# Attention written out without registers, and the routing of twelve of sixteen token blocks laid between its maximum chunks

## What is computed

```python
mod = (silu(c) @ wmod)                      # sa, ca, ga, sb, cb, gb, one row of 256 per batch
ga, gb = sign * max(|.|, 0.25)
h = layernorm(x) * (1 + ca) + sa
q, k, v = einsum(h, W_qkv)                  # 16 heads of 16
attn = softmax(causal(q @ k.T) / 4)
x = x + ga * ((attn @ v) @ W_o)
h = layernorm(x) * (1 + cb) + sb
probs = sigmoid(h @ router_w.T)             # 8 experts, widths 4 x 256 and 4 x 512
topw, sel = top_k(probs, 2)                 # weights divided by their sum + 1e-20
y = sum over the 2 experts of topw * (square(relu(h @ w1_e)) @ w2_e)
out = x + gb * y
```

## Time and profile before

| | us |
|---|---|
| median of three runs (lowest, highest) | 3000.57 (2999.84, 3001.91) |
| the profiled execution, its own time | 2998.05 |
| the span of the profiled execution, first to last instruction | 2996.4 |
| attention, first maximum chunk to last context | 245 to 2038 |
| routing stage | 2040 to 2445 |
| busy share of the span: PE, DVE, ACT, POOL | 87%, 75%, 57%, 21% |

### The profile page before, as it was taken

The page is one execution under the profiler, slowest core; times in us unless marked ns, Lnnn a source line. Parts: engine busy times, 40 slices in busy tenths (PEclk is TensorE's granted clock), DMA queues, the critical chain, the costliest instruction groups (busy, mean ns, idle before and its releaser), DMA issues. The chain is left out here.

```text
span 2996.4 us, 63588 instructions
## 1 busy us (share of the span) xinstructions
PE 2607.4 (87%) x16384; PEld 1391.3 (46%) x16384; DVE 2235.7 (75%) x5319; ACT 1718.0 (57%) x3557; POOL 643.7 (21%) x595
## 2 busy tenths in 40 slices
PE   6876999999999999999999999984566559999990
PEld 5761233333333333333333333323555559999990
DVE  6988988889788878887888988803666657777762
ACT  3650377767677667766776767782121227777770
POOL 2224111111100000000000000001454525565563
PEclk8995799999999999999999999996666669999995
DMA  4876535544530220220121120004444425555547
GB/s 152 284 274 184 186 138 175 183 153 161 184 121 29 70 70 10 72 70 28 51 69 37 41 69 13 9 15 154 146 159 141 148 79 81 89 95 90 88 76 239
DMA packets 229815, 332.44 MB, mean 111 GB/s; under 512 B 27472, under 2 KB 170064, under 8 KB 229456
## 3 DMA queue, kind: packets, MB, share of 16 engines
q1 hardware_dynamic: 165184, 200.83, 21.7%
q0 software_dynamic: 47376, 110.68, 14.2%
q10 hardware_dynamic: 16896, 16.78, 1.7%
HBM read 140.23 MB, written 187.20 MB: 109 GB/s over the span
## 5 line engine op out<-in xcount | busy, mean ns | idle before, releaser
L734 ACT ACTIVATE probs<-ps 128x512 f32<-128x512 f32 (+3 forms) x2560 | 1173.9, 540 | 612.4 <-PE ps L828 367.7
L763 DVE TENSOR_REDUCE early<-ps 128x1 f32<-128x512 f32 x1536 | 1005.0, 686 | 130.7 <-PE ps L806 111.2
L806 PE MATMUL ps<-ks,qs 96*128 96x512 bf16 (+3 forms) x2560 | 887.9, 364 | 58.1 <-POOL ks L697 30.6
L824 PE MATMUL ps<-qs,ks 99*128 99x512 bf16 (+3 forms) x2560 | 831.5, 351 | 30.6 <-ACT probs L734 19.1
L841 PE MATMUL ps<-probs,vs 128*32 128x512 f32 (+3 forms) x5120 | 601.2, 542 | 0.0
L806 PEld LDWEIGHTS ps<-ks,qs 96*128 96x128 bf16 x2560 | 248.0, 98 | 641.3 <-DVE early L763 227.3
L759 DVE CUSTOM_DVE_ANT_0 junk<-ps,causal 128x128 bf16<-128x128 f32 (+3 forms) x1024 | 487.6, 484 | 77.8 <-PE ps L806 66.2
L824 PEld LDWEIGHTS ps<-qs,ks 99*128 99x128 bf16 x2560 | 247.0, 98 | 329.2 <-ACT probs L734 196.0
L1413 POOL DMA_INDIRECT acc<-y,to x156 | 252.8, 1620 | 113.2 <-ACT y L1468 67.2
L1029 POOL MEMSET w_raw<- 128x2048 f32 x1 | 1.8, 1809 | 1177.7 <-POOLq L618 1177.7
L828 PE MATMUL ps<-ident_b,causal_b 128*128 128x128 bf16 x1024 | 215.3, 221 | 0.0
(11 more groups left out here) (177 smaller groups left out, 3232.9 us busy)
## 6 DMA issues: line engine op xcount, KB each, us to landing
rows_out<-empty POOLq DMA_DIRECT2D x129, 544.0 KB, 3.4
xg<-rows_out SPq DMA_DIRECT2D x39, 544.0 KB, 3.7
v_ones<-vt SPq DMA_DIRECT2D x16, 1024.0 KB, 6.1
vs<-v_ones SPq DMA_DIRECT2D x16, 1024.0 KB, 6.3
contexts<-ctx_out SPq DMA_DIRECT2D x64, 256.0 KB
q_parts<-parts SPq DMA_DIRECT2D x32, 384.0 KB, 3.8
k_parts<-parts SPq DMA_DIRECT2D x32, 384.0 KB, 4.4
qs<-q_parts SPq DMA_DIRECT2D x64, 192.0 KB, 3.1
```

The source lines that it names most:

```text
L734: nc.scalar.activation(probs[u % PB][:, h, q0:TB], bank(n % SB)[:, q0:TB], ACT.Exp, scale=SCALE).then_inc(exp_done[p], 1)
L763: nc.vector.tensor_reduce(early[:, h, t, k0 // CW:k0 // CW + 1], tile, AX.X, ALU.max).then_inc(max_done[p], 1)
L806: mm = nc.tensor.matmul(bank(4 + c % MS * (CW // 512), CW // 512)[:, m0:m0 + n], qs[p][0:STACK, h, t * P:(t + 1) * P], ks[p][0:STACK, h, k ...
L824: mm = nc.tensor.matmul(bank(n % SB)[:, q0:TB], ks[p][:, h, kt * P:(kt + 1) * P], qs[p][:, h, j * TB + q0:(j + 1) * TB], start=True, stop= ...
```

## The change

The attention (`attend`, in place of `block2`) is written out: no loops, every wait compares with a constant, and no increment stands behind a wait. Query and key tiles are now nine single heads that rotate (HR = 9), values two sets. `put_neg` writes per head, 12 DMAs in place of 3. POOL sets nine small tails of the key tiles in place of three large ones, and keeps two of its 129 filling DMAs in flight in place of one.

The work of `dispatch` for blocks 0 to 11 moves into the attention. A table of chunk numbers says where each piece stands: before chunk c of the maximum stream of group g, block n = g - 5 gets its piece. PE and DVE both walk through this stream, so the pieces take their PSUM banks from the same rotation of four (`take`, `freed`). Block 0 stands in step 4 (the stream of group 5), block 10 in step 14, and block 11 in step 15, which has no chunks of its own. ACT's pieces stand between its Exp instructions (`SCORES_TO`). The loads, the stores and the sends of these blocks are all issued by POOL. The inverses of the softmax sums are made for four blocks at once, before blocks 0, 4 and 8: POOL waits until all contexts of the batch are stored, loads the sums, waits for DVE's reciprocal at chunk 32, writes the inverses and only then fetches the block, which DVE needs at chunk 50. The modulation rows, inverse gates and first places are made by pieces in the stream of group 1 (step 0). The product with the inverse gate (L1055 on POOL) goes to DVE. `count` uses 5 matmuls in place of 11.

Blocks 12 to 15 stay in a stage of their own, `dispatch_rest`, with tiles of their own for each block, one set of inverses, x loaded and the residual stored by ACT's queue.

The diff, cut to its core:

```diff
-RING = 3
+HR = 9
+FILLS = (E * CAP + TB) // TB
+HIDDEN_BLOCKS = NBLK - BPB
+WIDEN, MOD, GATE_INVERSE, FIRST_PLACES = 20, (30, 34, 38, 42), (60, 80, 100, 120), 140
+INVERT, CONTEXT, PROJECT, RESIDUAL, STATISTICS, DEVIATION = 32, 50, (56, 60), (66, 70), 75, 79
+CENTRE, MODULATE, TRANSPOSE, ROUTE, PROBABILITY, RANK = 84, 90, (97, 101), 110, 120, 123
+SHARE, COUNT, OVER = 126, 136, 146
...
+                def load(a):
+                    g, h = divmod(a, HG)
+                    if a >= HR:
+                        sp.wait_ge(s_mm, NS * ((a - HR) // HG + 1))
...
+                def put_neg(g):
+                    sp.wait_ge(neg_done, 4 * (g + 1))
+                    for h in range(HG):
+                        for n in range(PARTS):
+                            sp.dma_start(qh[(HG * g + h) % HR][STACK + n:STACK + n + 1, :].rearrange(
+                                "a (t c) -> a t c", c=P), neg[g % 2][h * QT:(h + 1) * QT, n, :]).then_inc(neg_in, 16)
...
+                for g in range(NG):
+                    for a in range(HG * g + HR - HG, HG * (g + 1) + HR - HG):
+                        if HR <= a < HG * NG:
+                            load(a)
+                    if g:
+                        store(g - 1, BPB - 1)
+                        if g + 1 < NG:
+                            load_v(g + 1)
+                    for j in range(BPB - 1):
+                        store(g, j)
+                    if g + 1 < NG:
+                        put_neg(g + 1)
...
-                for p in range(RING):
-                    nc.gpsimd.memset(ks[p][STACK:STACK + PARTS, :, :], 1.0).then_inc(tables_set, 1)
+                for r in range(HR):
+                    nc.gpsimd.memset(kh[r][STACK:STACK + PARTS, :], 1.0).then_inc(tables_set, 1)
...
+                def inverses_of(b):
+                    for k in range(2):
+                        pool.wait_ge(ctx_stored[k], 64 * (NG // B) * (b + 1))
+                    if b:
+                        pool.wait_ge(inverse_out, 16 * b)
+                    nc.gpsimd.dma_start(sums[:, :], dens[...]).then_inc(sums_in, 16)
+                    pool.wait_ge(inverted, b + 1)
+                    nc.gpsimd.dma_start(inverses[...], sums[:, :]).then_inc(inverse_out, 16)
+                    pool.wait_ge(inverse_out, 16 * (b + 1))
...
+                for n in range(HIDDEN_BLOCKS):
+                    if n % BPB == 0:
+                        inverses_of(n // BPB)
+                    fetch(n)          # 2 contexts, 2 inverses, x
+                    name_tokens(n)
+                    send(n)           # 8 indirect DMAs
+                    store_over(n)
...
+                        for h in range(HG):           # ACT
+                            at = HG * u + h
+                            if n >= 0:
+                                if at == SCORES_TO[DEVIATION] + 6:
+                                    root(n)
+                                for k in range(KK):
+                                    if at == SCORES_TO[TRANSPOSE[k]] + 1:
+                                        turned(n, k)
+                                if at == SCORES_TO[ROUTE] + 1:
+                                    router_exp(n)
...
+                for g in range(NG + 1):               # DVE
+                    n = g - BPB - 1
+                    for c in range(NC):
+                        if g == 1:
+                            if c == WIDEN:
+                                widen()
+                            if c in MOD:
+                                mod_row(MOD.index(c))
+                            if c in GATE_INVERSE:
+                                gate_inverse(GATE_INVERSE.index(c))
+                            if c == FIRST_PLACES:
+                                first_places()
+                        if n >= 0:
+                            if c == INVERT and n % BPB == 0:
+                                invert(n // BPB)
+                            if c == CONTEXT:
+                                normalise_contexts(n)
...
+                            if c == OVER:
+                                over_gate(n)
+                        if g < NG:
+                            chunk(g, c)
+                    if g < NG:
+                        turn(g)
...
+                def take(kind, g, k):                 # PE
+                    slot = SLOT[kind, g, k]
+                    if slot >= MS:
+                        pe.wait_ge(*freed(slot - MS))
+                    return bank(4 + slot % MS)
...
+                def stream(g, c):
+                    n = g - BPB - 1
+                    if g == 1 and c in MOD:
+                        mod_rows(MOD.index(c))
+                    if n >= 0:
+                        if c in PROJECT:
+                            project(n, PROJECT.index(c))
+                        if c in TRANSPOSE:
+                            transposes(n, TRANSPOSE.index(c))
+                        if c == ROUTE:
+                            route(n)
+                        if c == COUNT:
+                            count(n)
+                    if g < NG:
+                        max_chunk(g, c)
...
+                normalise_contexts(0)                 # dispatch_rest, DVE
+                for m in blocks:
+                    if m + 1 in blocks:
+                        normalise_contexts(m + 1)
+                    gate_attention(m)
+                    residual(m)
+                    statistics(m)
+                    centre(m)
+                    if m:
+                        over_gate(m - 1)
+                    modulate(m)
+                    if m:
+                        choose(m - 1)
+                choose(blocks[-1])
+                over_gate(blocks[-1])
```

More of the change, by code:

```diff
@@ new lines, in attend @@
+        sums = sb("sums", [P, BPB * H * TB // P])
+        num, den, h2t = (w[:, :].rearrange("p (k t) -> p k t", k=KK) for w in work[0:3])
+        centred, over, gated, xres = (w[:, :].rearrange("p (t d) -> p t d", t=TT) for w in work)
+        row = sb("row", [P, TT, ROW])
+        stats = sb("stats_b", [P, TT, 6])
+        mv = sb("mv_b", [P, TT, 2])
+        rstd = sb("rstd_b", [P, TT])
+        choice = Choice(sb, "a")
+        tables_set, mask_set = sem("tables_set"), sem("mask_set")
+        empty_out = [sem(f"empty_out{k}") for k in range(2)]
@@ L670, in _ @@
-                load(0, 0)
-                load_v(0, 0)
-                load(1, 0)
-                load_v(1, 0)
-                put_neg(0, 0)
-                step(0, 0, before=False)
-                with sp.Fori(0, rounds - 1) as i:
-                    step(1, i)
-                    step(2, i)
-                    step(0, i + 1)
-                step(1, rounds - 1)
-                step(2, rounds - 1, ahead=False)
-                step(0, rounds, more=False, ahead=False)
-                store(0, rounds, BPB - 1)
+                def load(a):
+                    g, h = divmod(a, HG)
+                    b, hg = divmod(g, NG // B)
+                    if a >= HR:
+                        sp.wait_ge(s_mm, NS * ((a - HR) // HG + 1))
+                    rows = slice((hg * HG + h) * DK, (hg * HG + h + 1) * DK)
+                    toks = slice(b * S, (b + 1) * S)
+                    for side, src, same in ((qh[a % HR], q_parts, False), (kh[a % HR], k_parts, True)):
+                        for r0, n, other in ((0, 3, 0), (3 * DK, 2, 1), (5 * DK, 1, 2)):
+                            if same:
+                                s = src[rows, other:other + 1, toks].to_broadcast([DK, n, S])
+                            else:
+                                s = src[rows, 0:n, toks]
+                            sp.dma_start(side[r0:r0 + n * DK, :], s).then_inc(heads_in[a % HR], 16)
@@ L734, in step @@
-                            nc.scalar.activation(probs[u % PB][:, h, q0:TB], bank(n % SB)[:, q0:TB], ACT.Exp,
-                                                 scale=SCALE).then_inc(exp_done[p], 1)
-                step(0, 0, before=False)
-                with act.Fori(0, rounds) as i:
-                    step(1, i)
-                    step(2, i)
-                    step(0, i + 1)
-                context(0, rounds, BPB - 1)
+                                context(g, UNITS_TO.index(u - LAG + 1))
@@ L811, in max_turn @@
[L811 to L825 removed]
+                pe.wait_ge(w_in, 32)
@@ L886, in _, with dispatch_rest @@
-                step(0, rounds, more=False, ahead=False)
+                    stream(1, c)
+                for g in range(NG):
+                    step(g)
                 for u in range(NU - LAG, NU):
-                    p_v(0, rounds, u)
-def dispatch(nc, sb_, sem, bank, x, contexts, dens, inverses, rows_out, acc, wo_s, rw_s, ident, mod_t, gates,
-             w_in, w1, w2, w1_raw, w2_raw, raw_in, raw_zero, tiles):
+                    p_v(NG - 1, u)
+def dispatch_rest(nc, sb_, sem, bank, x, contexts, dens, inverses, rows_out, acc, wo_s, rw_s, ident, gates,
```

(9 more changed lines are left out.)

1181 lines of the change are left out of this document (642 added, 539 removed).

## The result

The changed kernel takes 2964.69 us in the median of four runs (2961.96 to 2966.86), against 3000.2 us in the runs of the kernel before beside it: 0.9883 of the time, 95% interval 0.987 to 0.9895. That is 35.5 us faster. Forecast were 132 us, 2868 us with a range from 2780 to 2940: the sign came, the size did not. The profiled span is 2964.8 us.

A forecast was written before the change was run, and what follows sets the result against it. The prediction took DVE to be nearly full in the attention and the routing stage to be bound by latency. Its terms summed to -132 us from 2998.05, 2866 us profiled and 2868 us in the median, range 2780 to 2940.

The forecast's parts named there:

- routing stage for 12 blocks: Stage after the attention: twelve blocks leave it, 118 of 404 us stay, -286 us (-300 to -270).
- blocks 0 to 10 in steps 4 to 14: Attention steps: DVE's gaps absorb part of 15.7 us a block, 11.3 us a step remain, +124 us (88 to 176).
- batch boundaries, over that: Steps 4, 8 and 12: DVE waits for sums and inverses, 10 to 11 us each, +32 us (12 to 60).
- modulation rows in step 0: DVE work that hid behind DMAs enters a step where DVE is full: +10 us (6 to 14).
- loops and registers: Attention written out: four loop rounds of 5.5 us and half a microsecond a step go, -29 us (-20 to -50).
- put_neg with 12 DMAs: Turn of each step: twelve DMAs in place of three, 0.6 us over for each of 16, +10 us (0 to 34).
- last step with block 11: Step without chunks, DVE free; PE gets 7 us and ACT 4 us of work: +8 us (4 to 12).
- start: Kernel start: nine smaller memsets in place of three, with the first `put_neg`: -1 us (-5 to +3).
- PE's share lies beside DVE's: Attention steps with a block: PE, up to four chunks ahead, does its pieces while DVE does its own; nothing charged.
- Rival C: Attention steps: PE's, DVE's and ACT's pieces run one after another, 27.4 us a step, 301 us, 3045 us in all; 5%.
- `put_neg`'s cover: Turn: three narrow units, about 7.5 us, lie beside the 8.1 to 9.6 us until the DMAs land.
- ACT's tables at 0: ACT's root in the steps: table changes of 2.6 us hidden where DVE is late, 0; at worst 29 or 59 us.

The follow-up runs named there:

- e10: The kernel of e1 word for word, run again on another chip: 2890.57 us.
- e5: The kernel before with only its attention loops written out and the increments behind waits left out: 2969.7 us, ratio 0.9901.
- e1: The changed kernel with the nine query tiles as one tensor, so `put_neg` needs 3 DMAs (6 where heads wrap) in place of 12: 2891.18 us.
- e11: e1 with each projection of a block cut to 4 products of 16 columns, the rest left out: 2861.78 us.
- e2: The changed kernel with Copy in place of Sqrt in ACT's root of blocks 0 to 11, so no table changes there: 2967.64 us.
- e13: e1 with later chunks for the pieces of blocks 0, 4 and 8 alone, the reciprocal at 46 in place of 32: 2867.2 us.
- e3: The changed kernel with SP storing a group's last context ahead of the next 24 loads in place of behind them: 2978.51 us.

## Why the prediction was wrong, point by point

The terms, with what the runs showed for each (from e10 where the difference to the changed kernel is `put_neg` alone):

```
term                                  forecast   measured
routing stage for 12 blocks             -286       -296    last Exp to the end, before and after
blocks 0 to 10 in steps 4 to 14         +124       +185    e10: (120.8 - 104.0) x 11
batch boundaries, over that              +32        +38    e10: (133.4 - 120.8) x 3; after 30
modulation rows in step 0                +10         +8    e10: 112.2 - 104.0
loops and registers                      -29        -30    e5
put_neg with 12 DMAs                     +10        +74    after less e1
unit 37 (not forecast)                     -        -20    e5 3.9, after 2.6 us, in 15 steps
last step with block 11                   +8        +11    100.5 - 89.6
start                                     -1         -3    first Exp, e10 333.9, before 337.3
sum                                     -132        -33    measured: -35.5
```

**The first step that failed** is "PE's share lies beside DVE's": the term for PE's pieces was put at nothing. The prediction read the earlier trace rows for DVE alone, "DVE is nearly full". The same row lists PE as busy for 104.25 of 107 us and DVE for 90.43. That PE can be four chunks ahead shifts its work and makes no room for more of it. Measured, a block's products take 6.7 us of PE's time in a step by their starts (8.2 as listed, by the groups of one step in e10: projections 3.8, transposes 1.3, router 1.8, counts 1.3), and e11 shows that most of it is paid: 2.6 us taken away, 2.1 given back. DVE's part, 11.3 us in the forecast, was not too small: PE stands 7.1 us more for DVE, 10.1 with all other standing. With PE's products a block costs 16.8 us and not 11.3, 61 us over eleven steps. Rival C had the right kind, pieces one after another, and the wrong size: 27.4 us took all three engines in series, while about half of DVE's 13.8 us lies beside PE's work.

**The second step that failed** is `put_neg`'s cover. The issue took 8.39 us where 5.8 to 7.3 were forecast, but the last DMA landed 9.5 us behind the first issue, inside the forecast's 8.1 to 9.6. The 0.6 us over go by the low end of that, which is 1.4 us too low. And the cover, three units or 7.5 us, is 1.9 us too large: PE had 5.6 us of work left behind SP's first issue, and stood for 3.9. Nothing was counted for the clock, which falls behind such a stand: for the next five microseconds products start 0.43 in place of 0.22 us apart. Together 74 / 16 = 4.6 us a step in place of 0.6. The forecast's upper bound, 34 us, was too low by half as well: it had no row for a stand of PE, and took none.

**What held.** The routing stage: 107.6 us are left from its first load (2304.84) to the experts' (2412.47), forecast 118. The loops, by e5, in size; in the kernel before three of the turns (by the start of their first instruction) stand out, 111.2 to 112.3 us behind the one before, not four, and the others give the rest. ACT's tables at 0, by e2. The boundaries' size, and by e13 the wait for the sums as their main cause, though the 24 loads took SP 14.4 us, 0.60 each, where 12 us were forecast. And the modulation rows. The turn's intervals were forecast at 105, 116 to 118 and 10 more at three steps. In e10, without the dear `put_neg`, they are 104, 121 and 134.

**What stays open.** Unit 37 lasts 4.0 to 4.3 us in the kernel before and 3.6 to 3.9 in e5 but 2.6 in the changed kernel, some 20 us in all. The turn's product now takes its bank in one stream with the chunks, but no run undid that alone. Also open are what the boundary steps of e13 still cost over their neighbours, 4.8 us each, and what differs between the places with and without the stop in units 32 and 33.

## What to carry to other kernels

Before work is laid into a stage, read the busy time of every engine in one window of that stage, and charge the new work to each engine by its own free time. An engine that is nearly full pays for most of every piece, even if another looks like the bound because others wait for it in short pieces. For PE, count by the distance between starts and not by the listed busy time, which hides short stops. A queue that hands small pieces to the critical engine costs by the number of its DMAs, at 0.6 to 0.7 us each here; join them before you hide them. And a wait of some 4 us in front of TensorE costs more than itself, since the products behind it run at the lower clock.

## What the runs showed of the hardware that was not expected

- SP issues a DMA without registers every 0.60 us (3 in 1.80, e10) to 0.70 us (12 in 8.39), though each of the twelve carries a quarter of the bytes (4 KB in place of 16): joining is worth more than the bytes say.
- After 3.91 us in which PE stood, 512-column products were listed at 0.61 to 0.63 us for about five microseconds, and at 0.38 after that.
- Products of 512 columns listed at 0.38 us start every 0.22 us (e10): a PE that is busy for 99.6% of a window by its list still stood for some 6 us in each step of 104.
- A change of ACT's table took 1.28 us and no more: no idle time of over 0.02 us stands before or behind any of 24 loads.
- A fetch of 512 KB issued 2.4 us behind a load of 1024 KB landed after 10.9 us in place of 6.6, and turned a saved wait into a longer one (e3).
- Four kernels on one chip lost some 6 us in each step with a block to a gap of 3.8 us on PE, in which ACT and DVE stood too, beside the last of POOL's eight indirect sends; the same four texts, run elsewhere, took 58 to 67 us less, with the kernel before at 2999 to 3000 us in every place. Texts that are to be compared belong on one chip, and a surprise that all kernels of one place share should be repeated elsewhere before it is explained.
